# A third token buffer, a new order of the attention blocks and gate products in column strips

## Chip, cores and metric

One core of a Trainium2 chip runs the kernel. The metric is the device time of the whole kernel in microseconds (us), inputs and outputs in the chip's memory. The median of three runs before the change is 517.7 us (517.23 to 518.28).

## What is computed

A cross attention without softmax (relu instead), then a mixture of eight experts of which each token uses two. All inputs are fp32. Cut to what matters:

```python
B, S, D = 2, 2048, 512            # 4096 tokens, 128 keys per batch
x = x + relu(logits(layernorm(x)) @ vp)
#   qp = relu(layernorm(x) @ Wq + bq); kp, vp = relu(ctx @ Wk + bk), relu(ctx @ Wv + bv)
#   logits = relu(qp @ kp.T) / sqrt(512) + mask
z = layernorm(x)
logits = z @ gate_w               # 8 experts
topv, topi = top_k(logits, 2); w = softmax(topv)
Y_e = (silu(z @ Wu[e]) * (z @ Wv[e])) @ Wo[e]
x = x + sum over the two chosen experts of w_k * Y_topi[k]
```

## The kernel before

**Attention stage.** 4096 tokens are worked on in 16 blocks of 256 (two tiles of 128). Precision is kept by splitting operands in a high and a low part (fp32r, the qT, qpT and lgT tiles with halves HI and LO): ScalarE writes the high half by a copy, VectorE the low half by a subtraction, and TensorE takes three matmuls per contraction chunk (`three`, L1164 to 1168). Each engine has its own queue in program order, and the order is written out by hand in a function `body(b)` per engine; semaphores tie them together. While TensorE works on block b, other steps of its neighbours run: `nxt` is b+1, `prv` b-1, `old` b-2 and `third` b-3.

**TensorE's block** (L1335 to 1358): the queries of b (four tiles m of 12 matmuls into banks psQ[0] and psQ[1], the ranks of `third` behind the first), the gate logits of `old` (L1250 to 1255: four fp32 matmuls with the 8 gate columns as the stationary operand, summed in one bank), the masks, the scores (into psS), the turn of the next tokens (transposes of xn into psT), the turn of the logits of `old`, the turn of the first half of the second norm's result z of `prv` (bank psZ), the attention product, the turn of the second half of z. Turns are matmuls on an identity (L1162).

**ScalarE** (L641 to 681) takes each query tile with relu and bias (L649), copies its high half (L554), normalises one token tile of `nxt` and both tiles of z of `prv` (L582, L599), takes the scores (L669), and copies what TensorE turned. **VectorE** (L977 to 1068) does the statistics of both norms (L826 to 838), one token tile's normalisation (L960), the low halves (L733), the logits with mask (L1045, L1047), the choice of two experts (`Choose`: L864 to 877), the place of each token in its expert's list (`Place`: L889 to 903), the weights (`Weigh`: L918 to 926) and the sum with the residual (`add_attention`, L815). **GpSimd** computes the powers for both norms (L505, L510) and for the weights, and scatters z rows to the experts' lists in DRAM (L491). **SyncE** loads tokens (two buffers, `xin`), masks and, in pieces over the blocks, the experts' weights.

**Block 14** also plans the first 16 tiles of the routed stage (`plan_lengths` to `plan_used`, chains of short dependent instructions on VectorE).

**Routed stage.** 78 tiles of 128 rows are gathered from the lists, taken through their expert (up, silu, product, down) and scattered back. The last blocks' gates, choices and places stand between its first tiles (L1376 to 1400). It begins when the last attention product is done.

## Time and profile before

| | |
|---|---|
| median of 3 runs | 517.7 us |
| profiled execution, whole | 514.76 us |
| its span, first to last instruction | 512.4 us |
| granted TensorE clock, mean | 0.972 |
| TensorE busy | 459.1 us, 90% |
| VectorE busy | 342.2 us, 67% |
| ScalarE busy | 278.7 us, 54% |
| GpSimd busy | 182.2 us, 36% |
| attention blocks 3 to 13, together | 151.21 us |

Busy is the time in which an engine had an instruction in work; a matmul's time reaches to the modelled end of its pipeline, so matmuls in a row overlap and the distance from start to start is what one costs. The same overlap, of some 0.08 us, is seen between short instructions of VectorE. The attention stage lies between about 19 and 248 us of the span.

### The profile page before, as it was taken

The numbers are of one execution on the slowest core, as the hardware profiler recorded it, in microseconds if no ns is written. First come the engines' busy times: TensorE is split into PE (matmuls) and PEld (weight loads), VectorE is DVE, ScalarE is ACT, GpSimd is POOL, SyncE is SP. The second block draws the span as 40 slices with busy tenths as digits, with TensorE's granted clock in tenths as the row PEclk, the third lists the DMA queues.
The fourth block names the chain that finished last, engine by engine and source line by source line (L and its number), as shares of the span: only waits on it lengthen the run. The fifth ranks groups of instructions, "written<-read, shape, count | busy, mean of one in ns | idle before, by whom it ended". The sixth has DMA issues, their size and how long they took to land.

```text
span 512.4 us, 10710 instructions
## 1 busy us (share of the span) xinstructions
PE 459.1 (90%) x3210; PEld 393.2 (77%) x3210; DVE 342.2 (67%) x1091; ACT 278.7 (54%) x590; POOL 182.2 (36%) x214
## 2 busy tenths in 40 slices
PE   5988999999999999989788698399997999899991
PEld 4847888888887878778577587299996889798980
DVE  2627788788888888787648567167664566566661
ACT  2735766766676767656556265166673344344430
POOL 2001124454545454435364423033332333333332
PEclk9999999999999999999999799699999899999996
DMA  7322225654444444436554878736644889889840
GB/s 265 117 56 88 62 76 166 229 168 169 167 167 144 147 158 143 154 121 202 173 189 155 299 225 323 256 125 205 213 133 124 290 262 290 282 269 286 275 150 0
DMA packets 54183, 93.79 MB, mean 183 GB/s; under 512 B 8305, under 2 KB 20593, under 8 KB 54130
## 3 DMA queue, kind: packets, MB, share of 16 engines
q1 hardware_dynamic: 42770, 59.02, 38.0%
q0 software_dynamic: 11360, 34.09, 17.7%
q8 instruction: 29, 0.48, 0.4%
q14 instruction: 24, 0.20, 0.2%
HBM read 51.78 MB, written 44.97 MB: 189 GB/s over the span
## 4 chain that ended last, share of the span: by engine, by line
PE 49%; issue 11%; DVE 11%; DMA 10%; SPq 9%; ACT 4%; POOL 3%; another core or an unknown queue 1%; POOLq 0%; DVEq 0%; ACTq 0%
PE psQ L1166 7%; PE psQ L1167 7%; PE psQ L1168 7%; PE psT L1162 6%; DMA wq<-z_dram 5%; PE psZ L1162 3%; PE psG L1254 3%; PE psO L1166 2%; SPq L439 2%; PE psS L1168 2%; DVE st L826 2%; PE psS L1166 2%; PE psS L1167 2%; POOL rstd L510 2%; SPq L420 2%
## 5 line engine op out<-in xcount | busy, mean ns | idle before, releaser
L733 DVE TENSOR_TENSOR qT<-psT,qT 128x512 fp32r<-128x512 f32 x110 | 75.4, 688 | 55.8 <-ACT qT L554 38.6
L1166 PE MATMUL psQ<-wuv,qT 128*128 x312 | 96.3, 309 | 0.6 <-DVE qT L733 0.6
L1167 PE MATMUL psQ<-wuv,qT 128*128 x312 | 89.6, 287 | 0.0
L1168 PE MATMUL psQ<-wuv,qT 128*128 x312 | 89.3, 286 | 0.0
L554 ACT ACTIVATE qT<-psT 128x512 fp32r<-128x512 f32 x110 | 63.9, 597 | 35.6 <-PE psT L1162 27.9
L1166 PE MATMUL psQ<-qT,wq 128*128 128x256 f32 x256 | 74.7, 292 | 1.0 <-ACT tl L565 1.0
L1167 PE MATMUL psQ<-qT,wq 128*128 128x256 f32 x256 | 72.4, 283 | 0.0
L1168 PE MATMUL psQ<-qT,wq 128*128 128x256 f32 x256 | 72.3, 282 | 0.0
L491 POOL DMA_INDIRECT z_dram<-zb x64 | 63.0, 985 | 19.6 <-issue 17.1
L1166 PEld LDWEIGHTS psQ<-wuv,qT 128*128 128x128 f32 x312 | 60.4, 194 | 5.4 <-issue 1.0
L1167 PEld LDWEIGHTS psQ<-wuv,qT 128*128 128x128 f32 x312 | 60.9, 195 | 0.0
L1168 PEld LDWEIGHTS psQ<-wuv,qT 128*128 128x128 f32 x312 | 60.8, 195 | 0.0
L623 ACT ACTIVATE gate_work<-psQ 128x128 f32<-128x128 f32 x78 | 21.6, 277 | 64.7 <-PE psQ L1168 64.3
L649 ACT ACTIVATE tq<-psQ,bq_sb 128x256 f32<-128x256 f32 x64 | 30.4, 475 | 41.0 <-PE psQ L1168 41.0
L1166 PEld LDWEIGHTS psQ<-qT,wq 128*128 128x128 f32 x256 | 48.9, 191 | 1.4 <-issue 1.4
L1167 PEld LDWEIGHTS psQ<-qT,wq 128*128 128x128 f32 x256 | 49.0, 191 | 0.0
L1168 PEld LDWEIGHTS psQ<-qT,wq 128*128 128x128 f32 x256 | 48.9, 191 | 0.0
L1162 PE MATMUL psT<-ident,wq 128*128 128x128 f32 x232 | 36.7, 283 | 13.0 <-DMA wq<-z_dram 12.9
L938 DVE TENSOR_TENSOR gate_work<-gate_work,psQ 128x128 f32<-128x128 f32 x78 | 22.4, 287 | 29.7 <-ACT gate_work L623 28.4
L510 POOL TENSOR_TENSOR rstd<-ve,minus_half 128x2 f32<-128x2 f32 x16 | 16.3, 1018 | 66.4 <-DVE ve L834 66.4
L1162 PEld LDWEIGHTS psT<-ident,wq 128*128 128x128 f32 x232 | 27.3, 145 | 15.4 <-DMA wq<-z_dram 14.2
L554 ACT ACTIVATE lgT<-psQ 128x128 fp32r<-128x128 f32 x78 | 21.7, 278 | 30.7 <-PE psQ L1162 16.3
(204 smaller groups left out, 1085.0 us busy)
## 6 DMA issues: line engine op xcount, KB each, us to landing
wq<-z_dram SPq DMA_DIRECT2D x58, 264.0 KB
xin<-in_x_dram SPq DMA_DIRECT2D x16, 512.0 KB, 4.0
xn<-z_dram SPq DMA_DIRECT2D x20, 264.0 KB
xin<-acc_dram SPq DMA_DIRECT2D x20, 256.0 KB
z_dram<-spare SPq DMA_DIRECT2D x18, 264.0 KB
x<-acc_dram SPq DMA_DIRECT2D x10, 256.0 KB, 5.2
acc_dram<-spare SPq DMA_DIRECT2D x9, 256.0 KB, 4.6
zb<-acc_dram SPq DMA_DIRECT2D x9, 256.0 KB
```

The costliest lines, as they stand in the source:

```text
L491: pool.indirect_dma_start(out=z_dram[k], out_offset=bass.IndirectOffsetOnAxis(ap=z_of(b)[:, t, ROW_COL + k:ROW_COL + k + 1].bitcast(U32), ...
L510: nc.gpsimd.tensor_tensor(rstd1[:, :], ve1[:, :], minus_half[:, :], ALU.pow).then_inc(rstd1_ready, 1)
L554: nc.scalar.activation(o, i, ACT.Copy).then_inc(s, 1)
L623: nc.scalar.activation(sil[:, t % 2, :], psQ[t % 2][:, 0:R], ACT.Silu).then_inc(silu_done, 1)
L649: nc.scalar.activation(tq[:, m % 2, :], psQ[m % 2][:, 0:BT], ACT.Relu, bias=bq_sb[:, m:m + 1]).then_inc(qp_relu, 1)
L733: nc.vector.tensor_tensor(o, a, b, ALU.subtract).then_inc(s, 1)
L938: nc.vector.tensor_tensor(s_tok[:, t % 2, :], sil[:, t % 2, :], psQ[t % 2][:, R:2 * R], ALU.mult).then_inc(s_ready, 1)
L1162: return pe.transpose(o, i, ident[0:n, 0:n])
L1166: pe.matmul(o, w[LO], a[HI], start=first, stop=False)
L1167: pe.matmul(o, w[HI], a[LO], start=False, stop=False)
L1168: return pe.matmul(o, w[HI], a[HI], start=False, stop=last)
L1254: ins = pe.matmul(ps_log, gw[:, c, :], zT[:, c, :], start=(c == 0), stop=(c == DC - 1))
```

## The change

It does these things.

- A third token buffer (over the memory of the turned context, which is free after the values are computed). Tokens are loaded two blocks ahead instead of one, masks one block ahead.
- TensorE turns the next tokens right behind the queries; masks and scores follow, then the gates of `old`, both turns of z of `prv` (the second one into bank psQ[0]), the attention product and the turn of the logits. The next block's queries wait for the copies of z.
- The gate matmuls write four strips of 32 rows of the bank, each from a strip of 32 columns of the array (8 of them gates, 24 zeros). The logits are then turned by a product with a 0/1 matrix `pick` that adds the four strips and keeps 8 columns.
- VectorE's and ScalarE's orders follow: the choice of `third` is taken at the head of a block, the next tokens' norm first, placing in one piece, and the experts' low halves behind the logits. GpSimd takes the first norm's power before the second's.
- Block 15, the last, keeps more of the old order: gates ahead of the scores, both z turns in psZ.

The core of the diff:

```diff
-            def body(b):
-                nxt = b + 1
-                if nxt.real:
-                    ge(sp, x1_ready, 2 * (nxt.n - 2) + 2)
-                    sp.dma_start(xin[:, nxt.p, :, :], x_blk[nxt.n]).then_inc(x_loaded[nxt.p], 16)
+            def load_x(b):
+                ge(sp, x1_ready, 2 * (b.n - XBUFS) + 2)
+                if b.n == 2:
+                    sp.wait_ge(v_done, 2)
+                sp.dma_start(x_of(b), x_blk[b.n]).then_inc(x_loaded[b.x], 16)
+
+            def load_mask(b):
                 ge(sp, s_done, b.n - 1)
                 sp.dma_start(mraw[:, b.p, :, :], m_blk[b.n % NB_G]).then_inc(m_loaded[b.p], 16)
+
+            load_x(Step(1))
+            load_mask(Step(0))
+
+            def body(b):
+                if (b + 2).real:
+                    load_x(b + 2)
+                if (b + 1).real:
+                    load_mask(b + 1)
...
+            nc.gpsimd.memset(gw[:, :, :], 0.0).then_inc(const_ready, 1)
...
+                if nxt.real:
+                    rstd1_of(nxt)
                 if prv.real:
                     rstd2_of(prv)
-                if nxt.real:
-                    rstd1_of(nxt)
...
-            def turned_z(b, t):
+            def turned_z(b, t, bank):
                 ge(act, z_turned, 2 * b.n + t + 1)
-                copy(zT[:, :, t * P:(t + 1) * P], psZ[:, :].rearrange("p (c k) -> p c k", c=DC), zT_ready)
+                copy(zT[:, :, t * P:(t + 1) * P], bank[:, :].rearrange("p (c k) -> p c k", c=DC), zT_ready)
...
-                if old.real:
-                    turned_z(old, 1)
-                for m in range(DC):
-                    queries(m)
-                if prv.real:
-                    norm2(prv, 0)
-                if old.real:
-                    gate_logits(old)
+                queries(0)
+                queries(1)
                 if nxt.real:
                     norm1(nxt, 1)
                 else:
                     expert_high(b)
+                queries(2)
+                queries(3)
                 if b.n == 0:
                     split_values()
-                ge(act, s_done, b.n + 1)
-                nc.scalar.activation(tl[:, :], psS[:, 0:BT], ACT.Relu, scale=SCALE).then_inc(s_relu, 1)
                 if nxt.real:
                     turned_x(nxt)
                 else:
@@ -675,8 +692,19 @@
                     turned_g(0)
                     turned_g(1)
                 if prv.real:
+                    norm2(prv, 0)
+                if not nxt.real:
+                    gate_logits(old)
+                ge(act, s_done, b.n + 1)
+                nc.scalar.activation(tl[:, :], psS[:, 0:BT], ACT.Relu, scale=SCALE).then_inc(s_relu, 1)
+                if prv.real:
                     norm2(prv, 1)
-                    turned_z(prv, 0)
+                if old.real and nxt.real:
+                    gate_logits(old)
+                if prv.real:
+                    turned_z(prv, 0, psZ)
+                if prv.real and nxt.real:
+                    turned_z(prv, 1, psQ[0])
                 if nxt.real:
                     expert_high(b)
...
+            nc.vector.tensor_reduce(pick[:, :], ident[:, :].rearrange("p (c s) -> p s c", s=STRIP)[:, 0:E, :], AX.X,
+                                    ALU.add).then_inc(conv_ready, 1)
+            dve.wait_ge(conv_ready, 5)
...
-                choose, put, weigh = Choose(old), Place(third), Weigh(third)
+                choose, put, weigh = Choose(third), Place(third), Weigh(third)
...
-                if prv.real:
-                    ge(dve, x1_ready, 2 * prv.n + 1)
-                    norm2.sums(0)
                 if third.real:
-                    put.ranks()
-                if prv.real:
-                    norm2.moments(0)
+                    choose.all()
+                if nxt.real:
+                    ge(dve, x_loaded[nxt.x], 16 * (nxt.n // XBUFS + 1))
+                    norm1.sums(0)
+                    norm1.sums(1)
+                else:
+                    expert_low(prv)
                 low(0)
+                if nxt.real:
+                    norm1.moments(0)
+                    norm1.moments(1)
+                    norm1.variance()
                 if prv.real:
                     ge(dve, x1_ready, 2 * prv.n + 2)
+                    norm2.sums(0)
+                low(1)
+                if nxt.real:
+                    norm1.shift()
+                    norm_x(nxt)
+                if prv.real:
                     norm2.sums(1)
-                if third.real:
-                    put.picked()
-                if prv.real:
+                    norm2.moments(0)
                     norm2.moments(1)
-                if third.real:
-                    put.rows()
-                if prv.real:
                     norm2.variance()
                 if third.real:
-                    put.write()
+                    put.all()
+                low(2)
                 if third.real:
                     weigh.all()
                 if ends_early:
                     dve.wait_ge(place, PLACE_STEPS * EARLY_NB)
                     plan_lengths(0)
-                low(1)
                 if prv.real:
                     norm2.shift()
                     keep_stats(prv)
+                low(3)
                 if ends_early:
                     plan_ends(0)
-                if nxt.real:
-                    ge(dve, x_loaded[nxt.p], 16 * (nxt.j + 1))
-                    norm1.sums(0)
-                low(2)
-                if nxt.real:
-                    norm1.moments(0)
-                    norm1.sums(1)
-                low(3)
-                if nxt.real:
-                    norm1.moments(1)
-                    norm1.variance()
-                if prv.real:
-                    expert_low(prv)
-                if ends_early:
-                    plan_experts(0)
-                if nxt.real:
-                    norm1.shift()
-                    norm_x(nxt)
-                if ends_early:
-                    plan_slots(0)
                 if b.n == 0:
                     for g in range(NBATCH):
                         dve.wait_ge(v_hi, g + 1)
                         sub(vp[:, LO, g, :], v_raw[g], vp[:, HI, g, :], v_lo)
...
+                for t in range(TPB):
+                    if nxt.real:
+                        turned_x(nxt, t)
+                    else:
+                        turned_g(t)
...
-                if old.real:
-                    choose.values()
                 ge(dve, lg_step, 3 * b.n + 2)
                 sub(lgT[:, LO, :], lg[:, :], lgT[:, HI, :], lg_step)
-                for t in range(TPB):
-                    if nxt.real:
-                        turned_x(nxt, t)
-                    else:
-
-                        turned_g(t)
-                    if t == 0 and not nxt.real:
-                        expert_low(b)
-                    if old.real and t == 0:
-                        choose.indices()
+                if ends_early:
+                    plan_experts(0)
+                    plan_slots(0)
+                if not nxt.real:
+                    expert_low(b)
+                elif prv.real:
+                    expert_low(prv)
                 add_attention(b, 0)
-                if old.real:
-                    choose.gaps()
-                    choose.one_hot()
+                if not nxt.real:
+                    Choose(old).all()
                 add_attention(b, 1)
...
+                ge(pe, zT_ready, 2 * (b.n - 1))
...
-            def turn_z(b, t):
+            def turn_z(b, t, bank):
                 ge(pe, z_ready, 2 * b.n + t + 1)
-                ge(pe, zT_ready, 2 * b.n + t)
+                ge(pe, zT_ready, 2 * b.n + (t if bank is psZ else 0))
                 for c in range(DC):
-                    ins = turn(psZ[:, c * P:(c + 1) * P], z_of(b)[:, t, c * P:(c + 1) * P])
+                    ins = turn(bank[:, c * P:(c + 1) * P], z_of(b)[:, t, c * P:(c + 1) * P])
                 ins.then_inc(z_turned, 1)
...
-                    ins = pe.matmul(ps_log, gw[:, c, :], zT[:, c, :], start=(c == 0), stop=(c == DC - 1))
+                    ins = pe.matmul(ps_log[c * STRIP:(c + 1) * STRIP, :], gw[:, c, :], zT[:, c, :], start=True, stop=True,
+                                    tile_position=(0, c * STRIP))
...
+                if b.n == 0:
+                    pe.wait_ge(conv_ready, 5)
                 for t in range(TPB):
-                    ins = turn(ps_logit[:, t, :], logT[:, t * P:(t + 1) * P], E)
+                    ins = pe.matmul(ps_logit[:, t, :], logT[:, t * P:(t + 1) * P], pick[:, :], start=True, stop=True)
...
                 queries(b)
-                if old.real:
-                    gates(old)
                 if b.n == 0:
                     values()
-                turn_masks(b)
-                scores(b)
                 if nxt.real:
                     turn_x(nxt)
                 else:
                     turn_g(0)
                     turn_g(1)
-                if old.real:
+                turn_masks(b)
+                if not nxt.real:
+                    gates(old)
+                scores(b)
+                if nxt.real:
+                    if old.real:
+                        gates(old)
+                    if prv.real:
+                        turn_z(prv, 0, psZ)
+                        turn_z(prv, 1, psQ[0])
+                    attend(b)
+                    if old.real:
+                        turn_logits(old)
+                else:
                     turn_logits(old)
-                if prv.real:
-                    turn_z(prv, 0)
-                attend(b)
-                if prv.real:
-                    turn_z(prv, 1)
+                    turn_z(prv, 0, psZ)
+                    attend(b)
+                    turn_z(prv, 1, psZ)
```

## Rows read from the trace of the kernel before

**Rows 1.** Windows by block: length; busy PE, PEld, DVE, ACT, POOL; clock; DMA.

```profile
40.09:53.59 13.50, 11.21 (x86) 10.23 (x84) 10.55 (x30) 8.43 (x17) 2.21 (x2) 1.00 0.26 80
66.80:218.01 151.21, 148.44 (x1092) 123.93 (x1091) 125.39 (x490) 103.64 (x204) 70.38 (x77) 1.00 0.48 159
121.98:135.88 13.90, 13.61 (x103) 11.28 (x101) 11.40 (x45) 9.32 (x19) 6.59 (x8) 1.00 0.44 155
218.01:233.59 15.58, 14.08 (x105) 11.46 (x103) 13.82 (x62) 9.34 (x18) 6.64 (x8) 1.00 0.48 156
```

**Rows 2.** TensorE's timeline, block 7: start, length, engine, line, what [idle before].

```profile
128.13 1.89 PE L1254 MATMUL psG<-zT_ctxT,gw 128*8 128x256 f32 x8
...
129.95 0.44 PE L1162 MATMUL psS<-ident,mraw 128*128 128x128 f32 x2
...
132.03 1.09 PE L1162 MATMUL psT<-ident,xn 128*128 128x128 f32 x8 [0.22 <-DVE xn L960]
...
133.05 0.29 PE L1162 MATMUL psG<-ident,logT 8*128 8x8 f32 x2
...
134.00 0.50 PE L1166 MATMUL psO<-vp,lgT 128*128 128x512 f32 x1
...
135.52 0.60 PE L1162 MATMUL psZ<-ident,zb 128*128 128x128 f32 x4
...
135.88 0.36 PE L1166 MATMUL psQ<-qT,wq 128*128 128x256 f32 x1
```

**Rows 3.** Timelines around the scores of block 6.

```profile
116.71 0.36 PE L1166 MATMUL psS<-qpT,kpT 128*128 128x256 f32 x1
...
118.41 0.38 ACT L669 ACTIVATE tl<-psS 128x256 f32<-128x256 f32 x1
...
119.66 0.41 DVE L733 TENSOR_TENSOR lgT<-lg,lgT 128x256 fp32r<-128x256 f32 x1
...
119.82 0.82 ACT L599 ACTIVATE zb<-x,nmr,rstd 128x512 f32<-128x512 f32 x1
...
120.12 0.50 PE L1166 MATMUL psO<-vp,lgT 128*128 128x512 f32 x1
```

**Rows 4.** ScalarE and VectorE, query tiles of block 7.

```profile
125.87 0.42 ACT L554 ACTIVATE qpT<-tq 128x256 fp32r<-128x256 f32 x1
...
129.19 0.43 DVE L733 TENSOR_TENSOR qpT<-tq,qpT 128x256 fp32r<-128x256 f32 x1 [0.22 <-ACT qpT L554]
```

**Rows 5.** VectorE's timeline, block 7, then the tile stage.

```profile
126.67 0.42 DVE L733 TENSOR_TENSOR qpT<-tq,qpT 128x256 fp32r<-128x256 f32 x1
...
127.01 0.15 DVE L838 SCALAR_TENSOR_TENSOR nmr<-mv,rstd 128x2 f32<-128x2 f32 x1
...
127.29 0.69 DVE L826 BATCH_NORM_STATS2 st<-xin 128x6 f32<-128x512 f32 x1
...
129.53 0.18 DVE L830 BATCH_NORM_AGGREGATE mv<-st 128x2 f32<-128x6 f32 x1
...
129.74 0.17 DVE L834 TENSOR_SCALAR ve<-mv 128x2 f32<-128x2 f32 x1
...
131.43 0.54 DVE L960 TENSOR_SCALAR xn<-xin,mv,rstd 128x512 f32<-128x512 f32 x1
...
273.15 0.24 DVE L864 MAX8 top_v<-psG 128x8 f32<-128x8 f32 x2
...
273.95 0.28 DVE L938 TENSOR_TENSOR gate_work<-gate_work,psQ 128x128 f32<-128x128 f32 x1
...
278.84 0.18 DVE L889 TENSOR_TENSOR pos<-psG,base 128x32 f32<-128x32 f32 x1
...
279.66 0.16 DVE L918 TENSOR_SCALAR den<-egap 128x2 f32<-128x2 f32 x1
...
280.13 0.15 DVE L809 CAST pad_i<-base 1x16 int32<-1x16 f32 x1
```

**Rows 6.** TensorE's timeline, the gates of block 14 in the first tile.

```profile
251.95 0.81 PE L1254 MATMUL psG<-zT_ctxT,gw 128*8 128x256 f32 x3 [1.57 <-DVE base L895]
```

67 lines of the change are left out of this document (36 added, 31 removed).

## The prediction

> **What bounds the kernel now.** I read the windows by block first, then TensorE's timeline through one block, then the timelines of ScalarE and VectorE around the waits of that block. The attention stage is 16 blocks of 256 tokens; a block is counted from the first matmul of its queries to that of the next. Blocks 3 to 13 take 151.21 us, 13.75 each, and TensorE is busy for 148.44 of them [rows 1]. VectorE is busy 11.4 us of each block, ScalarE 9.3. So this stage looks bound by TensorE. The reader should see two things that this share hides. First, in block 7 TensorE turns the next tokens at 132.03, after a wait of 0.22 for VectorE's normalised tokens [rows 2]. Second, the attention product begins as soon as VectorE has the low half of the logits: that subtraction runs from 119.66 for 0.41, to 120.07, and the product starts at 120.12 [rows 3]. The turning of z ahead of it begins at 133.27 in block 7 (133.05 and 0.22 for the logits) and needs 0.36, as at 135.52 to 135.88, yet the product starts only at 134.00, so some 0.37 us of each block is a wait inside a row that looks busy [rows 2]. The chain from the first score matmul to the product is 116.71 to 120.12, 3.41 us [rows 3]. The routed stage behind the attention follows tile by tile and has waits of its own; the change touches it in two gates and two turned logits.
>
> **What TensorE gains and loses.** In block 7 the gates take 128.13 to 129.95, 1.82 us for eight instructions, 0.23 each [rows 2]. The change gives each of the four contractions a strip of 32 columns of its own, so they may run side by side. Every fp32 matmul is two instructions here, and the two of one strip follow each other; if neighbours of different strips overlap, the chain is five slots of 0.23, 1.14 us. No row shows strips, so the bounds are 0.6 us (all four side by side: two slots and the end of the last, 0.38 less the overlap) and 1.82 (none). I take 1.14, the nearest sum with an order of instructions kept. The logits' turn costs 0.22 now (133.05 to 133.27), two instructions. After it, two true fp32 products with 128 stationary columns are four instructions. The turns of the tokens, each with a full stationary operand to load, follow each other 0.12 to 0.13 apart (eight in 1.02) [rows 2]. So bounds of 0.22 and 0.52; I take 0.46, since loading a full stationary operand four times is what is issued. A gain below 0.22 is excluded, as no fewer instructions run.
>
> **The new cover of the scores' input.** Now the scores follow the queries behind the gates and the masks, 2.02 us (128.13 to 130.15 with 0.20 of masks; gates 1.82), and that cover is long enough. After the change the cover is the turned tokens (0.96) and the masks (0.20). What it must cover is the last query's relu, copy and subtraction. In block 7 ScalarE copies the second query tile at 125.87 for 0.42; VectorE could subtract at 126.33, 4.35 after the block's start at 121.98. The last one starts at 129.19, 7.21 after the start, and ends at 129.62, so with a hand-over of 0.05 no score can start before 7.69 [rows 1, 4]. Queries, turning and masks end at about 6.15 (121.98 to 128.13) + 0.96 + 0.20 = 7.31, so 0.4 us of wait appears even if VectorE is free.
>
> **VectorE's run before the last subtraction.** It isn't free. The new order puts more in front of it. From the second subtraction on, in the new order: the subtraction 0.34 (126.67 to 127.01), the shift 0.08, the normalised tokens 0.46 (0.54 long, 0.08 of it overlapped with the next, as everywhere on this engine), one sum of the residual's norm 0.60 (0.69 long), its moments and variance 0.38 (0.09 and 0.21, 129.53 to 129.74, and 0.08 twice round), placing 0.82 (278.84 to 279.66), the third subtraction 0.34, weighing 0.47 (279.66 to 280.13), shift and kept stats 0.28 (127.01 to 127.29), the last subtraction with its hand-over 0.48. Sum 4.25 us [rows 4, 5]. Placing costs 0.82 in one piece because its steps wait for each other; interleaved, as now, the waits are filled, and that is some 0.35 lost. I take the price from the tile stage, where the same five instructions stand in one piece.
> When does this run start? VectorE itself is there early: counted from the start of the attention product, it adds the second half at 1.72 (the products' 1.51 and the hand-over) to 2.32, chooses in 0.80 (273.15 to 273.95), takes two sums of the next tokens (1.20), a subtraction (0.34), moments (0.38), a sum (0.60): 5.64. The second query tile arrives at 1.51 (134.00 to 135.52) + 0.46 + 4.35 = 6.32, so TensorE starts the run [rows 2, 4, 5]. ScalarE normalises one half of the tokens between the second and third query (0.82, as the same size at 119.82), from about 6.8 to 7.6 on that count; two relus and two copies of some 0.45 follow, to 9.4, still ahead of VectorE's last subtraction at 6.32 + 4.25 - 0.48 = 10.1 [rows 3].
>
> **Scores to product.** The 3.41 loses the max instruction that stands between cast and subtraction now, under 0.1. A second path comes beside it: both halves of z are turned before the product, and the second half waits for ScalarE's normalisation, which follows the relu: 118.41, 0.38 and 0.06 of hand-over, 0.82, 0.06, then 0.36 of turning, is 3.38 after 116.71, and a few hundredths to the product [rows 2, 3]. I take 3.40. The scores' twelve slots are 1.51 of it (ScalarE takes the result 1.70 after their start, their last matmul being some 0.28 long). Of the gates, 3.40 - 1.51 - 0.72 (two turns) = 1.17 us is free under this chain: side by side they cost nothing, but all that they gain beyond that brings nothing either.
>
> **The sum.** A block is 1.51 + 0.46 + 4.35 + 4.25 + 3.40 = 13.97 us. Blocks 3 to 13: 11 x 13.97 = 153.7 against 151.2, **+2.5** [rows 1]. The late token loads are gone in this sum, since a third buffer lets them be issued a block earlier; of their wait there is no term, as the norm of the next tokens is now first in the block and the load has a whole block of lead. Block 1 has no placing and no gates; its floor is 7.69 + 3.40 + 1.51 = 12.6 against 13.50: **-0.9** [rows 1]. Block 2 I leave as it is. Block 14 plans the first tiles; only the four dependent instructions of the lengths (4 x 0.21) stand ahead of the last subtraction, the others where VectorE waits for scores: 13.97 + 0.84 = 14.8 against 15.58, **-0.8** [rows 1, 5]. Block 15 loses a wait for placing and wins the earlier choice; even. Block 0: the tokens fill a wait of 0.8 but no longer lie behind the scores, **+0.1**. In the tile stage TensorE waits 1.57 us for VectorE's running bases before the gates of block 14 [rows 6]. VectorE gets there some 0.6 earlier and the gates are 0.7 shorter: **-1.0** of the possible 1.3; the bounds are 0, where a later wait takes it, and -2.5, with the gates of block 15 too. The start: one memset more on GpSimd's queue before the constants, and SyncE waits for it ahead of a 16 KB load, both before the first tokens land; nothing. Sum -0.1 us: 514.8 becomes 514.7 in the profiled execution (the span of 512.4 and what lies around it), and the median 517.7 becomes 517.6. The profiled one stands 2.9 below the median of the runs; I carry the difference over.
>
> **Rivals.** B, slower: the strips don't run side by side, or cost a drain at their borders. Then gates of 1.82 give 1.51 + 1.82 + 0.72 = 4.05 in place of 3.40, +0.65 in 13 blocks, and the tile stage's 0.7 is lost: 517.6 + 8.5 + 0.7 = 526.8. It decides from 1.17 us of gates on. A drain at both borders of 0.16 each (a matmul's 0.38 less its slot) adds 0.3 to 1.14: +0.3 x 13, 521.5; that is the likelier form. For it speaks that 1.14 leaves nothing to spare; against it, that the 8-row turns among 128-row ones at 133.05 show no gap [rows 2].
> The Trainium skill bears on this twice. "TensorE: Matmul & The Clock Gate", Part 3, says that matmuls in different column strips run concurrently and gives 2.38 times for three. "TensorEngine Tiling (Array Packing)", Key Properties, says that changing the tiling mode drains the engine. By the first the forecast stands, by the second alone rival B's milder form; no row of before shows either.
> C, faster: VectorE's run is shorter than its parts. If it weren't late at all, a block would be 7.69 + 3.40 + 1.51 + 0.46 = 13.06, 0.9 less, and the kernel at 517.6 - 0.9 x 12 = 506.8. A logits' turn at 0.22 gives -0.24 x 12 = -2.9. All of the other or half of the one is 514.7 to 512.2. For it speaks that the sum was made of start-to-start times, several of them from a stage where VectorE had neighbours; against it, that each such step was read at least once in one piece.
>
> **Chances.** A, as summed, within about 2 us of 517.6: 0.43, and of it 0.20 lies within 0.2% of 517.7 (1.0 us, about what a measurement of this kernel can tell from no change), 0.12 below and 0.11 above. B 0.28. C 0.29. So faster 0.41, same 0.20, slower 0.39. The range takes C down to 511.5 and B's milder form up to 523.5; beyond it lie the full forms, together 0.2.
>
> **What would show it.** Right: TensorE waits about 1.2 us before each block's first score matmul, for VectorE's subtraction of the queries; blocks 3 to 13 near 13.9, all alike, without the alternation of odd and even; gates at 1.1 or below from first to next; the turned logits at 0.45. VectorE with no wait between the second and the last query subtraction. Wrong: gates at 1.8 (B), or a wait before the scores of only 0.4 (C). I would be wrong altogether if the second turn of z into a query bank held up the next queries; on the count above its copy ends about 1.0 after the product's start, and the queries come 1.0 later.

## The result, and the profile after

The changed kernel took 520.35 us in the median of ten executions (518.18 to 522.98), the kernel before 516.41 (514.38 to 518.28) beside it on the same chip: a ratio of 1.0082, 95% interval 1.0054 to 1.011, so 0.8% slower. The forecast was 517.6 (511.5 to 523.5), no change in its likeliest case. The profiled execution of the changed kernel has a span of 516.4 us, against 512.4 before.

The same kernel, unaltered, was measured again, always beside the kernel before on the same chip: 0.9984 (0.9966 to 1.0003) in a second measurement, 1.0019 (0.9993 to 1.0045) and 1.0011 (0.9985 to 1.0036) in a fourth and a fifth, on three chips; the third is a single profiled execution. The kernel before was longer in the first measurement too, 516.41 us against 513.12 to 513.78 beside the later ones. So there are two things to explain: what the change did, which is nearly nothing in the sum, and what was added in the first measurement alone.

First the windows of the first profile, by block (length; busy PE, PEld, DVE, ACT, POOL; clock; DMA). The lines answer to [rows 1]: blocks 3 to 13, block 4, block 5, block 14.

```profile
67.16:224.03 156.87, 139.34 (x1114) 122.15 (x1113) 132.66 (x490) 99.72 (x204) 67.57 (x77) 1.00 0.46 154
81.10:95.06 13.96, 12.56 (x103) 11.11 (x103) 11.99 (x45) 9.01 (x18) 6.37 (x8) 1.00 0.49 160
95.06:109.69 14.63, 12.70 (x103) 11.10 (x103) 12.01 (x45) 9.10 (x19) 6.10 (x7) 1.00 0.59 202
224.03:240.26 16.23, 13.94 (x106) 12.19 (x105) 13.80 (x59) 9.30 (x18) 6.03 (x7) 0.89 0.33 117
```

The same view of the second profile of the same program, blocks 3 to 13 and block 14:

```profile
67.13:220.46 153.33, 138.06 (x1113) 122.09 (x1113) 132.99 (x490) 99.45 (x204) 67.54 (x77) 1.00 0.46 158
220.46:236.71 16.25, 14.01 (x105) 12.40 (x105) 13.56 (x58) 9.11 (x18) 6.01 (x7) 0.89 0.33 116
```

TensorE is busy 138 us of blocks 3 to 13 in the second profile where it was busy 148.44 [rows 1]: 0.94 us of each block's work is gone, most of it by the strips. The blocks are still 2.1 us longer in all, since TensorE now waits, and in the first profile 5.7 us longer. TensorE's timeline of one undisturbed block of the second profile shows where (start, length, engine, line, operation, tiles, idle before):

```profile
81.08 0.37 PE L1181 MATMUL psQ<-qT,wq 128*128 128x256 f32 x1
...
87.12 1.04 PE L1177 MATMUL psT<-ident,xn 128*128 128x128 f32 x8
88.00 0.38 PE L1177 MATMUL psS<-ident,mraw 128*128 128x128 f32 x2
89.75 0.39 PE L1181 MATMUL psS<-qpT,kpT 128*128 128x256 f32 x1 [1.37 <-DVE qpT L761]
91.38 0.64 PE L1270 MATMUL psG<-zT_ctxT,gw 128*32 128x256 f32 x8
91.95 0.66 PE L1177 MATMUL psZ<-ident,zb 128*128 128x128 f32 x4
92.62 0.65 PE L1177 MATMUL psQ<-ident,zb 128*128 128x128 f32 x4
93.16 0.50 PE L1181 MATMUL psO<-vp,lgT 128*128 128x512 f32 x1
...
94.66 0.51 PE L1288 MATMUL psG<-pick,logT 128*128 128x8 f32 x4
95.02 0.36 PE L1181 MATMUL psQ<-qT,wq 128*128 128x256 f32 x1
```

One wait in the block, 1.37 us before the scores, for VectorE's last query subtraction. The eight gate matmuls take 0.57 us from their first to the next matmul, where [rows 2] had 1.82.

**The books by block.** Each entry is the difference to the kernel before, in us, worked out from the starts of the queries in TensorE's timeline (blocks 0 to 15 and the first expert product) and the spans. The forecast stands beside it.

```
                     forecast  1st profile  2nd    4th    5th measurement
blocks 0 and 1        -0.8       +0.65     +0.65  +0.63  -0.89
block 2                0         -0.28     -0.28  -0.29  -0.29
blocks 3 to 13        +2.5       +5.66     +2.12  +2.25  +2.27
block 14              -0.8       +0.65     +0.67  +0.52  +0.49
block 15               0         -0.12     +0.58  -0.74  -0.44
tiles, to the end     -1.0       -2.55     -3.60  -0.67  -0.70
```

(The third profile, of a single execution, has blocks 3 to 13 at 153.36, +2.15. What is left to the difference of the spans is the start of block 0, -0.14 to +0.30.)

### The profile page after: what moved, and what is told of

Same layout as the page of the kernel before. It is cut to its first block, busy times and chain, and to the rows that moved or that the text cites. A ratio compares the mean times of both kernels' runs of the same rounds, so it can differ in the third digit from the quotient of the medians.

```text
span 516.4 us, 10775 instructions
## 1 busy us (share of the span) xinstructions
PE 447.6 (87%) x3242; PEld 393.7 (76%) x3242; DVE 351.9 (68%) x1092; ACT 273.9 (53%) x590; POOL 178.8 (35%) x215
## 4 chain that ended last, share of the span: by engine, by line
PE 57%; DVE 17%; issue 6%; SPq 6%; ACT 5%; DMA 5%; another core or an unknown queue 2%; POOL 0%; POOLq 0%; DVEq 0%
PE psQ L1181 8%; PE psQ L1183 8%; PE psQ L1182 8%; PE psT L1177 5%; PE psS L1181 4%; PE psS L1183 4%; PE psQ L1177 3%; PE psS L1182 3%; DVE qpT L761 3%; PE psO L1181 2%; DVE st L856 2%; PE psO L1183 2%; PE psO L1182 2%; PE psZ L1177 2%
## 5 line engine op out<-in xcount | busy, mean ns | idle before, releaser
L761 DVE TENSOR_TENSOR qT<-psT,qT 128x512 fp32r<-128x512 f32 x110 | 74.3, 689 | 51.6 <-ACT qT L577 32.0
L514 POOL DMA_INDIRECT z_dram<-zb x64 | 64.1, 1002 | 39.3 <-DVE zb L876 20.3
L1181 PEld LDWEIGHTS psQ<-qT,wq 128*128 128x128 f32 x256 | 49.5, 193 | 1.5 <-issue 1.4
L1182 PEld LDWEIGHTS psQ<-qT,wq 128*128 128x128 f32 x256 | 49.6, 194 | 0.1
L1183 PEld LDWEIGHTS psQ<-qT,wq 128*128 128x128 f32 x256 | 49.5, 193 | 0.0
L1181 PE MATMUL psS<-qpT,kpT 128*128 128x256 f32 x64 | 20.0, 312 | 19.0 <-DVE qpT L761 19.0
```

The costliest lines, as they stand in the source:

```text
L514: pool.indirect_dma_start(out=z_dram[k], out_offset=bass.IndirectOffsetOnAxis(ap=z_of(b)[:, t, ROW_COL + k:ROW_COL + k + 1].bitcast(U32), ...
L761: nc.vector.tensor_tensor(o, a, b, ALU.subtract).then_inc(s, 1)
L1181: pe.matmul(o, w[LO], a[HI], start=first, stop=False)
L1182: pe.matmul(o, w[HI], a[LO], start=False, stop=False)
L1183: return pe.matmul(o, w[HI], a[HI], start=False, stop=last)
```

## Experiments

Sixteen runs were made: ten altered kernels, two of them twice, and the changed kernel itself four times. Each group of them ran on one chip with the kernel before, five chips in all. Ratios are to that kernel before.

**1. The gates and the logits' turn as they were, all else changed.**

```diff
-                    ins = pe.matmul(ps_log[c * STRIP:(c + 1) * STRIP, :], gw[:, c, :], zT[:, c, :], start=True, stop=True,
-                                    tile_position=(0, c * STRIP))
+                    ins = pe.matmul(ps_log[0:E, :], gw[:, c, 0:E], zT[:, c, :], start=(c == 0), stop=(c == DC - 1))
```

> The changed kernel with its gate products as they were before: all four summed in one place on 8 columns, and the logits turned by two transposes. It tells what the strips are worth in the new order. Rows of the changed kernel show the strips' gates in 0.56 us (91.42 to 91.98) where the old ones took 1.82, and the turned logits in 0.36 where the old took 0.22. Theory: the scores-to-product stretch of 3.42 us hides gates up to 1.17 us, so undoing the strips costs 1.51 + 1.82 + 0.72 - 3.42 = 0.63 us in each of 13 blocks less 0.14 for the logits, about +6.5 us, and some 1 to 2 us in the first tiles: 527 to 529 against 520.4. Rival: gates are hidden at any length by the wait for VectorE ahead of the scores, since that wait stays where it is: 520 to 521.

Measured 527.06 us, 1.0259 (1.023 to 1.0289). Each of blocks 3 to 13 takes 14.76 to 14.78, 162.51 us in all. TensorE's timeline of one block:

```profile
91.53 0.39 PE L1181 MATMUL psS<-qpT,kpT 128*128 128x256 f32 x1 [1.37 <-DVE qpT L761]
...
93.16 1.89 PE L1270 MATMUL psG<-zT_ctxT,gw 128*8 128x256 f32 x8
94.98 0.66 PE L1177 MATMUL psZ<-ident,zb 128*128 128x128 f32 x4
...
95.83 0.47 PE L1181 MATMUL psO<-vp,lgT 128*128 128x512 f32 x1
```

The wait before the scores is the same 1.37. From the scores to the product are now 4.30 us, and they are all TensorE's work: 1.63 of scores, 1.82 of gates, 0.85 of two turns. With strips it is 3.41, set by the other engines: in the block shown above VectorE's last subtraction of the logits ends at 93.10, and the product starts at 93.16. So the strips pay 0.84 a block (14.78 less 13.94), and of the 1.25 us that they save on the gates some 0.36 is saved for nothing. Rival B priced its full form at 0.65 a block; its mechanism is shown here, at a somewhat higher price. Neither border of the strips costs anything: the gates start 0.21 after the last score matmul with strips and 0.22 without, and the turn behind them starts before their last one has ended in both.

**2. The strips alone in the kernel before.**

```diff
+        pick = sb("pick", [P, E])
...
-                    ins = pe.matmul(ps_log, gw[:, c, :], zT[:, c, :], start=(c == 0), stop=(c == DC - 1))
+                    ins = pe.matmul(ps_log[c * STRIP:(c + 1) * STRIP, :], gw[:, c, :], zT[:, c, :], start=True, stop=True,
+                                    tile_position=(0, c * STRIP))
```

> The kernel before with one part of the change alone: gates in column strips and logits turned by the 0/1 matrix. In the old order the gates stand ahead of the masks and scores. Theory: the gates shrink from 1.82 to 0.56 us, but the scores cannot start before 7.69 us after the block's start, where they start at 8.17 now, so only 0.48 us of the 1.26 is won in a block, and in odd blocks the wait for the next tokens takes that again; 0.14 us of longer logits lies under an existing wait. About -0.2 to -0.5 us a block, -2.5 to -6 us: 510.5 to 514 against 516.4. Rival: TensorE is 98% busy there, so all of 1.26 us a block is won, 13 blocks and two gates in the tiles: -18 us, 498.

Measured 511.26 us, 0.9955 (0.9926 to 0.9985). The time was as expected, the place was not: blocks 3 to 13 take 151.27 us, within 0.1 of the 151.21 before, with 13.44 and 14.00 in turn. TensorE's timeline there:

```profile
100.21 0.64 PE L1260 MATMUL psG<-zT_ctxT,gw 128*32 128x256 f32 x8
101.75 0.38 PE L1172 MATMUL psS<-qpT,kpT 128*128 128x256 f32 x1 [0.54 <-DVE qpT L737]
104.11 1.09 PE L1168 MATMUL psT<-ident,xn 128*128 128x128 f32 x8 [0.67 <-DVE xn L966]
...
106.21 0.50 PE L1172 MATMUL psO<-vp,lgT 128*128 128x512 f32 x1 [0.17 <-DVE lgT L737]
```

TensorE works 9.6 us less (138.87 against 148.44) and waits as much more: for the queries, for the tokens, for the logits. The old order was already at VectorE's pace in these blocks, however busy TensorE looked. The gain is block 15's 1.24 us (13.74 against 14.98) and the tiles'.

**3. The third buffer alone, and with the strips, in the old order.** The first has the loads of the changed kernel (tokens two blocks ahead), the second also the edit of experiment 2.

> The kernel before with the third token buffer alone (tokens loaded two blocks ahead, masks one). Theory (the buffer gives little by itself: in the kernel before, the load was waited for in two blocks only): blocks 3 to 13 fall by 0 to 0.8 us in all from 151.2, and the time is 0 to 1 us below the kernel before. Rival (the buffer is what carries the changed kernel's gains): 2 us or more below. Second rival (the loads two blocks ahead get in the way of the experts' loads): slower by 0.5 us or more.

Measured 512.72 us, 0.9979 (0.9961 to 0.9998). Blocks 3 to 13 fall by 0.78 to 150.43, as forecast: blocks 5 and 13, whose turned tokens came late before, are 13.86 and 13.89 now.

> The kernel before with the third token buffer and the column strips, in its old order. The strips alone gave 0.9955 and kept blocks 3 to 13 at 151.3 us, every second block being held by VectorE's tokens; the buffer alone gave 0.9979. Theory (each helps at its own place): 0.992 to 0.995, blocks 3 to 13 at 150.4 to 151.3. Rival (the buffer sets free what the strips gain, so that the turned tokens are no longer waited for): blocks 3 to 13 at 147 or less and 0.985 to 0.988, as good as the moved orders.

Measured 510.84 us, 0.9943 (0.9927 to 0.9959), blocks 3 to 13 at 151.26. The rival, that buffer and strips set each other free, is out. What is left is that the moved orders had to bring the rest, and they brought 153.3.

**4. VectorE's run before the last subtraction made shorter.** In the changed kernel, placing, shift, kept stats and (block 14) the lengths are put behind it:

```diff
-                if third.real:
-                    put.all()
                 low(2)
...
-                if prv.real:
-                    norm2.shift()
-                    keep_stats(prv)
                 low(3)
+                if third.real:
+                    put.all()
+                if prv.real:
+                    norm2.shift()
+                    keep_stats(prv)
```

> The changed kernel with VectorE's placing, the second norm's shift and the kept stats (and the planner's lengths in block 14) moved from ahead of the last query subtraction to right behind it; weighing stays ahead. Nothing else. Theory: VectorE's run in front of that subtraction (4.25 us summed, seen as 1.38 us of TensorE waiting before each block's scores) is what the block is made of; without 1.1 us of it the scores start some 0.8 us earlier and VectorE is late by 0.2 us with the logits instead: about 13.4 us a block where the changed kernel has 13.96 to 14.6, and 2 us less in block 14, so -8 to -10 us: 510 to 513. Rival: the block is paced by the choice of experts and the ranks behind the first query tile, which waits in four blocks; then nothing moves: 520.

Measured 504.56 us, 0.9815 (0.9781 to 0.9849). Blocks are 13.08 (143.90 in all), the wait before the scores 0.51. This is far more than expected, and beats both kernels. It takes 1.10 us out of the run and gets 0.86 back. The next experiment moves placing alone (and the lengths that hang on it):

> The changed kernel with placing alone (and the lengths of block 14, which wait for it) moved behind the last query subtraction; the shift and kept stats stay ahead of it. Theory (a block is 1.51 + 0.36 + 4.35 + VectorE's run + 3.40, the run being 4.25 with all of it): the run loses 0.82, so blocks 3 to 13 fall from 13.94 to 13.1-13.2 us each (144.5 to 145 in all), TensorE's wait for the queries' subtraction from 1.37 to 0.55-0.65, and the time is 0.8 to 1 us above that with all of it moved: 505 to 506 at 513.6 for the kernel before. Rival (placing costs less than its 0.82 there, and the shift and the kept stats carry the rest): 13.4 us or more a block.

Measured 507.58 us, 0.9887 (0.987 to 0.9905), blocks at 13.35. The time came 2 us above the expectation and the block 0.2 above. Both engines in that block:

```profile
86.25 0.42 ACT L577 ACTIVATE qpT<-tq 128x256 fp32r<-128x256 f32 x1
86.40 0.17 DVE L864 TENSOR_SCALAR ve<-mv 128x2 f32<-128x2 f32 x1
...
86.71 0.43 DVE L761 TENSOR_TENSOR qpT<-tq,qpT 128x256 fp32r<-128x256 f32 x1
...
87.81 0.42 DVE L761 TENSOR_TENSOR qpT<-tq,qpT 128x256 fp32r<-128x256 f32 x1
...
88.28 0.38 PE L1180 MATMUL psS<-qpT,kpT 128*128 128x256 f32 x1 [0.79 <-DVE qpT L761]
```

VectorE is ready for the third subtraction at 86.48, but ScalarE's copy of that tile ends only at 86.67: ScalarE has normalised half of the tokens in between, from 85.05 for 0.81, and had waited 0.56 before that for VectorE's shift, which follows the second subtraction. From the second subtraction, at 84.52, to the scores are 3.76 us instead of 4.35; of placing's 0.82, 0.23 is lost to this new wait. In experiment 4's first kernel the third subtraction stands in the same wait. So the next limit is ScalarE's order, where that normalisation stands ahead of two queries' copies. That moving it would help is not shown: no run moved it.

**5. The lengths of block 14 alone moved behind the last subtraction.**

```diff
-                if ends_early:
-                    dve.wait_ge(place, PLACE_STEPS * EARLY_NB)
-                    plan_lengths(0)
...
                 low(3)
                 if ends_early:
+                    dve.wait_ge(place, PLACE_STEPS * EARLY_NB)
+                    plan_lengths(0)
```

> The changed kernel with the five instructions that plan the lengths moved behind the last query subtraction, in block 14 alone. Theory (the 0.82 us of the lengths stand on the chain of block 14, and the longer wait that they make for TensorE before the scores, 2.25 us, is what lets the clock fall there): block 14 goes from 16.23 to 14.2-14.8 us, the scores of it from 2.46 to 1.7, and the whole is 1.5 to 2.5 us shorter than the changed kernel. Rival (the planning is hidden, block 14 is long for its other steps): block 14 stays at 15.8 or more and the time within 0.5 us of the changed kernel. Blocks 3 to 13 as in the changed kernel by both (156-157 us).

Measured 513.35 us, 1.0002 (0.9976 to 1.0028). Block 14 falls to 14.50 us. The windows around its wait, first of the changed kernel (second profile), then of this one (same columns as above; the clock is the third from the end):

```profile
228.00:230.00 2.00, 0.01 (x1) 0.01 (x1) 1.79 (x13) 1.34 (x3) 0.72 (x1) 0.97 0.00 0
230.00:232.00 2.00, 2.00 (x9) 2.00 (x10) 1.75 (x5) 0.19 (x1) 1.39 (x3) 0.50 0.34 135
```

```profile
228.00:230.00 2.00, 0.63 (x6) 0.60 (x6) 1.83 (x13) 1.69 (x4) 0.45 (x1) 1.00 0.00 0
230.00:232.00 2.00, 2.00 (x22) 1.46 (x20) 1.86 (x7) 0.86 (x2) 1.54 (x2) 1.00 0.34 135
```

After the wait of 2.24 us the granted clock is 0.50, the lower of its two levels (1.2 and 2.4 GHz), and the scores, 1.63 us elsewhere from their first matmul to the gates', take 2.86. After a wait of 1.37, without the lengths, it stays at 1.00. So the theory held for block 14: it is 1.57 to 1.75 us shorter than in the unaltered kernel's five profiles, though a wait of 0.31 for the logits is new in it. The wait before the scores is 0.88 shorter, which leaves 1.0 to 1.2 for the clock, an estimate from these figures. But the 1.5 to 2.5 us that were expected of the whole didn't show: the unaltered kernel's 0.9984 to 1.0019 hold this one's 1.0002 in their middle. Block 15 is 15.46 us here, with 1.44 of it a wait for VectorE's choice before the ranks. Blocks 14 and 15 together are 29.96, against 30.34, 30.34, 30.61, 31.09 and 31.81 in the unaltered kernel. VectorE plans behind the scores. Where the clock falls only late in them (scores of 1.81 and 1.96 us), TensorE is slow afterwards and waits just 0.55 and 0.64 for the choice; where the scores themselves are slow (2.13, 2.40, 2.86) it waits 0.93, 1.16 and 1.44; here, where TensorE isn't slow at all, the planning shows in full. So part of what block 14 wins comes back in block 15.

**6. Where the first profile lost 3.5 us.** In it four of the blocks 3 to 13 take 14.63 or 14.66, and five 14.06 to 14.11. Here are the end of block 4's product and what follows, in the first profile:

```profile
93.51 0.60 ACT L577 ACTIVATE zT_ctxT<-psQ 128x512 f32<-128x512 f32 x1
94.27 0.69 DVE L845 SCALAR_TENSOR_TENSOR x<-psO,xin 128x512 f32<-128x512 f32 x1 [0.19 <-PE psO L1183]
94.46 0.40 PE L1183 MATMUL psS<-vp,lgT 128*128 128x512 f32 x1
95.71 0.69 DVE L845 SCALAR_TENSOR_TENSOR x<-psS,xin 128x512 f32<-128x512 f32 x1 [0.75 <-PE psS L1183]
...
97.01 0.19 DVE L907 TENSOR_TENSOR onehot<-iota_e,top_i 128x32 bf16<-128x32 uint32 x1
...
97.26 0.18 PE L1230 MATMUL psG<-onehot,before 128*128 128x16 bf16 x1 [0.53 <-DVE onehot L907]
```

and in the second, of the same program, where all stands 0.03 to 0.04 us earlier up to the delays:

```profile
93.32 0.60 ACT L577 ACTIVATE zT_ctxT<-psQ 128x512 f32<-128x512 f32 x1
94.16 0.69 DVE L845 SCALAR_TENSOR_TENSOR x<-psO,xin 128x512 f32<-128x512 f32 x1
94.43 0.40 PE L1183 MATMUL psS<-vp,lgT 128*128 128x512 f32 x1
94.86 0.69 DVE L845 SCALAR_TENSOR_TENSOR x<-psS,xin 128x512 f32<-128x512 f32 x1
...
96.16 0.19 DVE L907 TENSOR_TENSOR onehot<-iota_e,top_i 128x32 bf16<-128x32 uint32 x1
96.53 0.18 PE L1230 MATMUL psG<-onehot,before 128*128 128x16 bf16 x1
```

TensorE's last product matmul ends at 94.86 in the first and at 94.83 in the second. The addition that waits for it starts 0.85 after that in the first, 0.03 in the second. ScalarE's copy, which also waits for TensorE, is 0.15 late too. From there on VectorE's choice is 0.85 late and, since it has only 0.18 us in hand (its end at 96.35, the ranks at 96.53), TensorE waits 0.53 for it and the block is 0.69 longer.

My first theory was that VectorE is caught when it goes into the wait for TensorE with an instruction still running, and that a small step between the two additions guards against it:

```diff
                 add_attention(b, 0)
...
+                else:
+                    ge(dve, x1_ready, 2 * b.n + 1)
+                    nc.vector.tensor_copy(scr[:, :], x1[:, 0, 0:2])
                 add_attention(b, 1)
```

> The changed kernel with one tiny VectorE instruction (a copy of two columns) put between the two additions of the attention product, waiting for the first addition's result. In four of blocks 3 to 13 VectorE starts the second addition 0.85 us after TensorE's last matmul of the product, where 0.05 is normal, and TensorE then waits 0.5 us for the ranks. Theory A, that it comes of VectorE sitting in a wait for TensorE's signal while the first addition runs: the tiny step takes VectorE past the time of the signal, the four late starts go, and the time falls by about 2 us less 0.1 us a block: 519 to 520. Theory B, that the signal itself is late on TensorE's side: the late starts stay, and the step costs up to 0.1 us a block: 520.5 to 522.

Measured 514.48 us, 1.0021 (0.999 to 1.0051), blocks 3 to 13 at 153.34 and no late start. The second addition starts 0.14 after TensorE's last product matmul, behind the copy. That looked like a full success of the theory. The next two say otherwise. The copy without the wait:

> The changed kernel with a small copy between VectorE's two additions that reads constants and waits for nothing. Theory 1 (the late start comes whenever VectorE goes into the wait for TensorE's second signal while its first addition is still running; the copy with a wait on the addition's end puts that wait behind it): the copy without a wait leaves the engine's queue in the wait at nearly the same moment, so late starts stay (blocks of 14.6 us among those of 14.1) and the time is within 1 us of the changed kernel. Theory 2 (any instruction between the two breaks it, since the wait belongs to the instruction that follows an addition): all blocks 3 to 13 at 13.9-14.0, 153-154 us in all, some 3 us below the changed kernel.

Measured 512.88 us, 0.9992 (0.9968 to 1.0017), 153.42, no late start either; and experiment 5, whose blocks 3 to 13 are the changed kernel's to the letter, had 153.31 and none. So the changed kernel itself was run again, twice on one chip, and once more on each of two others:

> The changed kernel itself, unaltered, once more. In its profile four attention products have a second addition that starts 0.85 us after TensorE's last matmul, and four more 0.14-0.16 after it; in the kernel with only block 14's planning moved there was none, though the code of blocks 3 to 13 is the same. Theory P (the late starts belong to this program): again about four blocks of 14.6 and the rest at 14.1, blocks 3 to 13 at 156-157 us, time 1.006 to 1.010 of the kernel before. Theory X (they belong to single executions or to a chip, not to the program): here blocks 3 to 13 may come at 153.3 with no late start, and the time at 1.001 to 1.005, the rest of its excess being block 14's 2 us.

> The changed kernel, unaltered, a third profile. Theory P (late starts belong to the program): the same blocks (4, 7, 8, 12) at 14.6 us as in its first profile. Theory X (they belong to single executions or a chip): another set of blocks, or none; with none, blocks 3 to 13 take 153.3 us. Block 14 at 16.0-16.3 us by both, with a granted clock under 0.65 right after its wait.

> The changed kernel, unaltered, in a fourth measurement. Theory X (the first measurement, 1.0082, was of a chip or of executions with late signals; without them the kernel is even with the one before): ratio 0.997 to 1.002, blocks 3 to 13 at 153.3 us. Theory P (the second measurement was the exception): ratio 1.006 to 1.010, with blocks of 14.6 us among 14.1. A value between 1.002 and 1.006 would say that both occur within a chip.

> The changed kernel, unaltered, in a fifth measurement. Theory X (late signals are the exception, and without them the kernel is even with the one before): ratio 0.997 to 1.003, blocks 3 to 13 at 153.3 us. Theory R (they recur on some chips): ratio 1.006 to 1.010 here or with the same chance in a later one, blocks 3 to 13 at 156 us or more in the profile.

Measured: 512.83 us, 0.9984 (0.9966 to 1.0003); one execution of 515.76; 514.71 us, 1.0019 (0.9993 to 1.0045); 513.69 us, 1.0011 (0.9985 to 1.0036). Blocks 3 to 13 take 153.33, 153.36, 153.46 and 153.48 us, and the two additions of each product start 0.03 or 0.04 after TensorE's last matmul in all of them. Theory X holds: the late starts don't belong to the program. In the first measurement they can't have been a single execution's accident, since all ten executions took 518.18 us or more (the profiled one is the shortest of them), where the highest of the 36 in the later measurements is 517.18. Beside the unaltered kernel, the one with the copy on the same chip:

> The changed kernel with the small copy between the two additions, beside the unaltered one on the same chip. Theory N (the copy changes nothing where no signal is late): the two ratios agree within 0.3%, blocks 3 to 13 at 153.3-153.5 in both. Theory G (the copy itself gives what its first run seemed to give, 3.5 us): 0.5 to 0.7% below the unaltered kernel on this chip.

Measured 514.77 us, 1.0015 (0.9983 to 1.0047), blocks 3 to 13 at 153.54: level with the unaltered one's 1.0011. The copy does nothing where nothing is late, and my first theory is without support; whether it would guard on a chip with late starts wasn't seen, for none of the later ones had them. What makes TensorE's signals late there stays open.

**7. Both remedies together,** experiment 4 with the small copy, on two chips:

> Both remedies at once: placing, the shift, the kept stats and the lengths behind the last query subtraction, and the small copy between the two additions. Theory (two separate causes: VectorE's run before the subtraction, and the late start of the second addition): with the run shortened the choice is never what TensorE waits for unless the start is late; blocks 3 to 13 fall by no more than 0.5 us from the 143.9 of the first remedy alone, since no late start showed in it, and the time is within 1 us of it (some 9.5 us below the kernel before, 503.5 to 505.5 at 513.8 for that one). Rival (the copy gives its own 3.5 us wherever it stands): 9 to 13 us below, that is 500.5 to 502.5.

> The fastest version (placing, shift, stats and lengths behind the last subtraction, small copy between the additions) once more. Its blocks 3 to 13 have 0.5 us of wait at the queries' subtraction, and nothing in it should hang on a chip: ratio 0.979 to 0.984 by both theories, blocks 3 to 13 at 143.9. If late signals come here too, every block in which they do is up to 0.2 to 0.5 us longer, and the ratio rises to 0.985 or more.

Measured 504.16 us, 0.9812 (0.9784 to 0.9839), and 505.75 us, 0.9852 (0.9821 to 0.9882), blocks 3 to 13 at 143.94 and 144.02. The second ratio lies above the 0.979 to 0.984 expected, though its profile has no late start; the blocks are as expected, and where the rest lies is open. The copy adds nothing here either. Block 1 is 12.42 in both profiles and 13.90 in experiment 4's, but that is the clock of block 0, below, and not the copy, since it comes and goes in the unaltered kernel too.

## Why the prediction was right or wrong

**The block's sum held, by two small errors that cancel.** Forecast were 1.51 + 0.46 + 4.35 + 4.25 + 3.40 = 13.97 us, measured 13.94: product 1.50 (93.16 to 94.66), logits 0.36, queries to the second subtraction 4.32 (81.08 to 85.40), run 4.35, scores to product 3.41. The logits are 0.10 too dear and the run 0.10 too cheap; that this comes out even is luck, the mechanism is not. Blocks 3 to 13 were to cost +2.5 and cost +2.1 to +2.3 in three of the four measurements. VectorE's run can be checked step by step in its timeline, second profile (start, length):

```profile
85.40 0.42 DVE L761 TENSOR_TENSOR qpT<-tq,qpT 128x256 fp32r<-128x256 f32 x1
...
85.81 0.54 DVE L996 TENSOR_SCALAR xn<-zT_ctxT,mv,rstd 128x512 f32<-128x512 f32 x1
...
86.27 0.68 DVE L856 BATCH_NORM_STATS2 st<-x 128x6 f32<-128x512 f32 x1
...
86.87 0.38 DVE L860 BATCH_NORM_AGGREGATE mv<-st 128x2 f32<-128x6 f32 x2
...
87.36 0.18 DVE L925 TENSOR_TENSOR pos<-psG,base 128x32 f32<-128x32 f32 x1
...
88.18 0.42 DVE L761 TENSOR_TENSOR qpT<-tq,qpT 128x256 fp32r<-128x256 f32 x1
...
89.28 0.42 DVE L761 TENSOR_TENSOR qpT<-tq,qpT 128x256 fp32r<-128x256 f32 x1
```

Placing takes 0.82 in one piece (87.36 to 88.18), as priced; moments and variance 0.49 where 0.38 stood, the one step that was too short by 0.1. No wait stands between the second and the last subtraction, and TensorE waits 1.37 before the scores (about 1.2 was named). All blocks are alike within 0.03.

**The gates and the logits were mis-sized, both on the dear side.** Forecast 1.14 and 0.46, measured 0.57 and 0.36. The lower bound of 0.6, all four strips side by side, was the true value. It moved nothing, since below 0.93 the gates are free (3.41 less scores of 1.63 and turns of 0.85; the forecast had 1.17, with scores of 1.51 and turns of 0.72). By what the Trainium skill says in "TensorE: Matmul & The Clock Gate", Part 3, that matmuls in different column strips run concurrently, the trace agrees: 3.2 times for four strips in fp32. The drain of "TensorEngine Tiling (Array Packing)", Key Properties, shows at neither border.

**The step that failed against the first measurement** is the one in the part on VectorE's run, "VectorE itself is there early". It was counted with hand-overs of 0.05 only, and no wait for the ranks was given a term. With such hand-overs there is none, but the margin is 0.18 us. In the kernel before, the additions start 0.36 to 0.46 us behind TensorE's last matmul anyway, being queued behind VectorE's own work. The last step of the choice stands behind the first of them only, and has 1.2 us in hand before the ranks (block 7 and the start of block 8):

```profile
135.34 0.68 DVE L815 SCALAR_TENSOR_TENSOR x<-psO,xin 128x512 f32<-128x512 f32 x1
...
136.01 0.18 DVE L877 TENSOR_TENSOR onehot<-iota_e,top_i 128x32 bf16<-128x32 uint32 x1
...
137.39 0.18 PE L1214 MATMUL psG<-onehot,before 128*128 128x16 bf16 x1
```

The change puts the second addition and the whole choice directly between TensorE's product and TensorE's ranks. A hand-over of 0.85 then costs 0.69 of a block, four times, and shorter delays 0.14 each in five further blocks: 3.5 us, 0.7%, where 0.77% part 1.0082 from the 1.0005 mean of the other three. That such delays cost the kernel before nothing isn't shown: no profile of it was taken beside the first one, 0.85 is more than its 0.36 to 0.46, and it was itself 2.6 to 3.3 us longer in that measurement than in the later ones. So the late starts account for 3.5 of the 5.6 to 7.5 us by which the changed kernel's 520.35 exceeds its later medians; how much of the ratio is theirs stays open, as does their cause.

Nor are they all that failed. The first profile stands 4.0 us above the one before, where the forecast had -0.1. Of these 4.1 us, blocks 3 to 13 are 3.2 and blocks 0, 1 and 14 are 2.9, most of it the clock, for which the forecast had no term (next two paragraphs); the tiles gave 1.6 back. That the later ratios come near the forecast of no change is therefore partly luck: in the second profile the same 2.9 us are made up by tiles that are 2.6 us better than forecast.

**Blocks 0 and 1, forecast -0.8: the mechanism right, a condition missed.** Where the clock stays up it was -0.89. In most executions it doesn't. The forecast named 0.1 us for what no longer lies behind block 0's scores; it is a wait of 1.77 us for VectorE's logits (0.84 before). The windows from 38 us on, of the second profile and of the fifth measurement's:

```profile
38.00:40.00 2.00, 1.40 (x4) 1.11 (x5) 0.52 (x2) 0.10 (x1) 0.00 (x0) 0.69 1.06 315
40.00:42.00 2.00, 2.00 (x8) 1.71 (x7) 1.23 (x2) 0.74 (x1) 0.00 (x0) 0.50 0.09 34
```

```profile
38.00:40.00 2.00, 1.50 (x7) 1.24 (x8) 0.92 (x2) 0.30 (x1) 0.00 (x0) 1.00 0.97 286
40.00:42.00 2.00, 2.00 (x18) 2.00 (x17) 2.00 (x4) 0.92 (x2) 0.00 (x0) 1.00 0.05 15
```

The same wait, and the clock falls to 0.50 in one and stays in the other: 1.5 us between them. It fell in ten of the fourteen profiles of kernels with the changed order, and in none of the four of the old order, whose wait is 0.84. The forecast had no term for a clock.

**Block 14, forecast -0.8, was +0.5 to +0.7.** The lengths were priced right, 0.84 against 0.82. What failed is the step that stopped at their price: 1.37 and 0.82 of waiting are nearly all of one wait of 2.25, and behind it the clock falls. Experiment 5 shows both parts.

**Block 15 and the tiles.** The tokens' late loads were rightly given no term. Block 15 scatters from -0.74 to +0.58, and with it TensorE's wait for the one-hot choice behind VectorE's planning (0.64 to 1.44): the earlier the clock falls in block 14's scores, the longer it is (experiment 5). In the first tile the gates still wait for VectorE's bases:

```profile
254.82 0.64 PE L1270 MATMUL psG<-zT_ctxT,gw 128*32 128x256 f32 x8 [1.77 <-DVE base L931]
```

That is the fourth measurement, against 1.57 in [rows 6]: the gates are shorter, the wait is not. With block 15's gates, the tiles win 0.7 in two profiles and 2.6 to 3.6 in two others; 1.0 was forecast, and where the rest comes from I can't say, since the long wait of that stage, 10.5 to 11.4 us for z from DRAM around 330 us, moves with the loads.

**The rivals.** C described what experiment 4 then made: a block of 13.06, "if it weren't late at all". It is 13.08 with placing moved, and 504.56 us. The forecast put it to chance whether the steps were shorter than read; it would have been better to ask which of them need not stand there.

## What to carry to other kernels

A wait that ends on another engine's chain can't be shortened by giving the waiting engine less to do: count the chain between the two hand-overs (here VectorE's 4.35 us of small steps), and move out of it what nobody needs yet. Here that was worth 1.9% on two chips and 1.5% on a third, while buffer and strips together in the old order were worth 0.6%, and the new order with them gave most or all of that back (0.9984 beside it on the same chip, 1.0005 in the mean of three). Give each hand-over a margin; a step with 0.2 us in hand is on the path as soon as one signal comes late. When one measurement and one profile seem to name a cause, run the unaltered kernel again before believing the experiment that makes it vanish.

## What the runs showed of the hardware

- Four column strips of 32 with fp32 operands and 256 moving columns run side by side: eight instructions in 0.57 us, against 1.82 one after the other, with no loss at the borders to full-array matmuls.
- In one measurement, on one chip, VectorE started its additions 0.08 to 0.87 us after TensorE's last matmul instead of 0.03 to 0.05, and ScalarE a copy 0.19 to 0.23 after it; this was seen around the attention product, from block 4 on. In none of the thirteen other profiles of the new order did they.
- TensorE's granted clock after a wait, TensorE having been busy before: 2.24 to 2.25 us, it fell to 0.50 in nine of nine profiles (block 14), in some at once and in others up to 1.4 us after the wait; 1.76 to 1.78, in ten of fourteen (block 0); 1.74 and 1.75 in block 14 of the two kernels with strips in the old order, in neither; 1.37, in none of the blocks 3 to 13. A fall cost 1.0 to 1.2 us in block 14, by the estimate of experiment 5, and 1.5 in blocks 0 and 1.
